# State-space layer with spiking layer on one core: ScalarE's next decay ahead of its weighing of the third tile

## The reference

```python
dA = jnp.exp(dt_t[:, :, None] * A)          # A: one number for each of the 16 states
h = dA * h + dB[:, None, :] * x_t[:, :, None]
y = jnp.einsum('bdn,bn->bd', h, C_t) + Dskip * x_t
```

## Time and profile before

| | |
|---|---|
| median of 3 runs | 5144.43 us |
| the profiled execution | 5153.22 us |
| its span, first to last instruction | 5151.5 us |
| mean granted TensorE clock, share of full | 0.872 |
| VectorE busy | 4268.4 us (83%) |
| GpSimd busy | 4212.7 us (82%) |
| TensorE busy, matmul | 3777.7 us (73%) |
| ScalarE busy | 3045.5 us (59%) |

### The profile page before, as it was taken

How to read it: one execution, slowest core, us unless ns; L and a number is a source line. 1 busy time by engine, 2 the same in 40 slices (tenths; PEclk the granted TensorE clock), 3 DMA queues, 4 the chain that set the end, 5 groups by cost and what they waited for, 6 DMA issues and landing times.

```text
span 5151.5 us, 73020 instructions
## 1 busy us (share of the span) xinstructions
PE 3777.7 (73%) x20244; PEld 2377.5 (46%) x20244; DVE 4268.4 (83%) x3342; ACT 3045.5 (59%) x3906; POOL 4212.7 (82%) x3338
## 2 busy tenths in 40 slices
PE   4677777777777777777777777777777777777765
PEld 1444444444444444444444444444444444444443
DVE  0888888888888888888888888888888888888894
ACT  2566675656656566565665566665666566665552
POOL 1889898878888788887888779888898888888892
PEclk8899888888988889888889888888988898889977
DMA  2212112221222212221222212211221122212210
GB/s 68 77 51 79 57 51 68 69 75 48 63 61 69 67 45 74 59 70 57 62 62 67 60 54 74 63 57 57 74 68 49 57 77 62 60 48 72 63 38 19
DMA packets 189403, 315.20 MB, mean 61 GB/s; under 512 B 51992, under 2 KB 164120, under 8 KB 188960
## 3 DMA queue, kind: packets, MB, share of 16 engines
q1 hardware_dynamic: 188960, 310.06, 20.2%
HBM read 171.87 MB, written 20.05 MB: 37 GB/s over the span
## 4 chain that ended last, share of the span: by engine, by line
PE 24%; issue 22%; DVE 21%; ACT 17%; POOL 11%; SPq 2%; DMA 1%; DVEq 1%; POOLq 0%; ACTq 0%
DVE st L918 15%; PE ht L1038 9%; POOL st L528 8%; ACT decay L674 6%; PE work L1015 4%; PE work L1123 3%; DVE y L901 2%; SPq L402 2%; ACT L660 2%; ACT L815 1%; ACT weighed L685 1%; PE work L1111 1%; PE work L1065 1%; POOL xb L582 1%; PE work L1104 1%
## 5 line engine op out<-in xcount | busy, mean ns | idle before, releaser
L918 DVE TENSOR_TENSOR_SCAN st<-decay,st 128x1536 f32<-128x1536 f32 x768 | 2573.8, 3351 | 328.9 <-ACT decay L674 276.7
L528 POOL TENSOR_TENSOR st<-xc,bbc 128x1536 f32<-128x1536 f32 x768 | 2659.5, 3463 | 75.6 <-DMA bbc<-brow 70.4
L1038 PE MATMUL ht<-ident,st 128*128 128x128 f32 x9216 | 1442.6, 312 | 595.2 <-DVE y L901 581.6
L674 ACT ACTIVATE decay<-dt,neg_a 128x1532 f32<-128x1532 f32 x768 | 1182.3, 1539 | 1063.7 <-DVE st L918 1063.0
L1038 PEld LDWEIGHTS ht<-ident,st 128*128 128x128 f32 x9216 | 1226.1, 162 | 874.8 <-DVE y L901 582.6
L573 POOL TENSOR_TENSOR y<-y,weighed 128x512 f32<-128x512 f32 x768 | 1016.7, 1324 | 474.7 <-ACT weighed L685 468.6
L901 DVE SCALAR_TENSOR_TENSOR y<-ht,ct,y 128x512 f32<-128x512 f32 x1536 | 1067.0, 735 | 42.6 <-PE ht L1038 40.5
L685 ACT ACTIVATE weighed<-ht,ct 128x512 f32<-128x512 f32 x768 | 526.0, 685 | 467.9 <-PE ht L1038 465.8
L1015 PE MATMUL work<-tri,conv_w 96*32 96x384 f32 x4608 | 500.5, 575 | 126.4 <-issue 74.5
L1065 PE MATMUL work<-xn,win 128*128 128x480 f32 x768 | 373.3, 612 | 40.1 <-POOL xn L509 36.4
L1070 PE MATMUL work<-xn,win 128*128 128x384 f32 x768 | 329.8, 581 | 20.3 <-ACT xb L660 19.1
(11 more groups left out here) (91 smaller groups left out, 3543.5 us busy)
## 6 DMA issues: line engine op xcount, KB each, us to landing
bbc<-brow SPq DMA_DIRECT2D x192, 768.0 KB, 4.4
tri<-xhp SPq DMA_DIRECT2D x2304, 50.0 KB, 2.0
xin<-in_x_dram SPq DMA_DIRECT2D x48, 384.0 KB, 3.3
out_dram<-ot SPq DMA_DIRECT2D x48, 384.0 KB, 4.0
brow<-xp SPq DMA_DIRECT2D x48, 24.0 KB, 1.5
win<-in_L_conv_W_in_dram SPq DMA_DIRECT2D x1, 1024.0 KB
wo<-in_L_conv_W_out_dram SPq DMA_DIRECT2D x1, 512.0 KB
w1s<-in_L_conv_W_dram SPq DMA_DIRECT2D x1, 256.0 KB, 3.2
```

The source lines that it names most:

```text
L528: u = g.tensor_tensor(slot, xc[:, kq % 2, :, :], bbc[:, piece_slot(kq, p), n % PIECE, :].unsqueeze(1).to_broadcast([P, DC, T]), ALU.mult)
L674: a.activation(decay[:, :, 1:], dt[:, (k + ahead) % 2, :, 1:], ACT.Exp, scale=neg_a[:, n:n + 1]).then_inc(s_dec, 1)
L918: v.tensor_tensor_scan(state, decay[:, :, :].rearrange("p c t -> p (c t)"), state, 0.0, ALU.mult, ALU.add).then_inc(s_scan, 1)
L1038: last = t.transpose(ht[:, m, c * P:(c + 1) * P], st[:, j, c, m * P:(m + 1) * P], ident[:, :])
```

## The change

In each step ScalarE's call `next_decay(s)` moves from behind the two weighing calls to ahead of them. It stays behind the early evacuations and ahead of the late ones. No instruction is added or removed, and the lists of the other engines are the same.

```diff
                     if s == 12 and PRE2 in do:
                         normalise_input()
+                    next_decay(s)
                     if s >= Y_LAG and main:
                         weigh(s - Y_LAG, 0)
                     if s < Y_LAG and post:
                         weigh(NS - Y_LAG + s, 1)
-                    next_decay(s)
                     for kind, name in late:
                         if kind in do:
                             evacuate(name, kind)
```

## The result

The changed kernel takes 5361.94 us (median of 4 runs, 5352.25 to 5378.45), the kernel before, on the same chips, 5145.53 us. The ratio is 1.042, 95% interval 1.039 to 1.046. The forecast was 5335 us; the change costs 216 us where 190 were expected. Its profiled execution has a span of 5350.5 us.

The account below looks back on a forecast made before the run. VectorE (83% busy) and GpSimd (82%), which every state passes through, were taken to bound the kernel. An estimated 4.0 us for each of 47 block heads, 188 us, on 5153.2 us, less 8.8, gave 5335 us; range 5215 to 5450.

Parts of the forecast that it names:

- The sign and the mechanism: Slower, chance 0.92: the weighing stands behind the decay, delaying GpSimd's sum and the scan input queued behind it.
- The marks that I named: Profile signs: weighing 1.47 us after each decay, fewer decay waits, new waits on GpSimd's lines 528, 535 and its sum.
- well over 1000: GpSimd's wait for ScalarE's weighing was to grow from 468.6 us to more than 1000 us.
- my 3.8: Cost in us of the block worked through: 1.3 + 2.6 + 1.3 - 3.4 + 0.9 + 1.1, with +0.9 for late evacuations.
- the 4.0 us for all blocks: Estimated mean cost per block, between 1.5 and 6.5 us; with 47 block heads, 188 us.
- The loop of 10.60 us for two plain scans: Plain steps: decay, weighing, GpSimd's sum, carry and scan input take 10.60 us per two scans, where it was 9.94.
- The three gaps up to scan 6: Three plain gaps after the block's head, at 10.60 us for two, add 1.3 us.
- The head, 1.3 + 2.6 us: Block start: scan 1 is 1.3 us late behind state 15's sum; scan 3 loses 2.6 more behind the small normalising instructions.
- The stall that gives back 3.4 us: At TensorE's last convolution group, scan 7 is only 1.8 us late instead of 5.2, so 3.4 us come back.
- The tail, 1.1 us: Block end: state 11's sum and scan 14 move by 1.47 us, scan 15 gets part back: +1.1 us.
- The lock: VectorE's line 927 against GpSimd's scan inputs: 51 us back or 66 us cost, left out of the sum.
- the kind case: Rival: all 21 long instructions of line 927 shrink, giving 51 us back, 5282 us; chance 0.15.

Follow-up runs that it names:

- the middle steps: The kernel before, with ScalarE's decay ahead of the weighing in steps 2 to 10 of each block alone; 5126.77 us, ratio 0.9955.

## Why the prediction was right, and where its terms were off

*The sign and the mechanism* were right. The late weighing holds GpSimd's sum, and the next scan input stands behind it. The marks that I named are in the profile: the weighing 1.48 us behind the decay (2682.53 and 2684.01), the statistics that wait for the sum, scans that wait for lines 528 and 535, decay waits down. The same order with only the sum moved is 213 us faster, which shows the mechanism apart from the waits' names. One mark failed in size: GpSimd's wait for the weighing rose to 832.8 us, in 521 places, not "well over 1000". Why it stays below is not shown.

*The number* was helped by luck. In the block of the earlier trace rows the terms are measured at 1.4 + 3.1 + 1.4 - 3.5 + 1.0 + 1.4 = 4.7 us, with some rounding, against my 3.8, and the mean block k = 0 costs 3.6. But the 4.0 us for all blocks were an estimate without a sum behind it, and they hold (4.1) only because lines 873, 881, 884 and 927 give back 12 to 31 us in each of k = 1 to 4 over the eight images. Without that the blocks cost 3.6, 4.2, 6.5, 7.7, 6.6 and 4.7 us, for the stall of blocks k = 0 is missing in k = 2 to 4.

*The loop of 10.60 us for two plain scans* is measured at 5.67 + 4.96 = 10.63 us. I took it for steps of 5.3 us; it shows as a wait in every second step. The three gaps up to scan 6 cost 1.4 us in this block, as forecast (1.3), but over all blocks gaps 3 to 5 together give 15 us back: line 881 returns 22 there, and the stall of blocks k = 5 another 19.

*The head, 1.3 + 2.6 us.* Measured in that block: 8.15 - 6.78 = 1.4 and 12.99 - 9.93 = 3.1 us. The excess in the second is the step from the last small instruction (2695.93 and 0.20 us) to ScalarE's first of the three (2696.60), 0.47 us, for which I had nothing. In the mean of blocks k = 0 the two are 1.2 and 2.7. Over all blocks, gaps 0 and 2 cost 59 + 96 us, and gap 1 gives 15 back. Undone, the head returns 145, and alone it costs 114, so it is half to two thirds of the result.

*The stall that gives back 3.4 us.* In the block of the earlier trace rows the gap of 8.5 us is gone (now 5.0), in the mean of blocks k = 0 gap 6 gives back 2.6 us, and over all blocks 30. But the run with the head in the old order did not bring it back. That it hangs on when the first convolution group starts is therefore not shown, and the middle steps give it back too.

*The tail, 1.1 us,* was too small. Gap 13 costs 74 us, gap 14 gives 12 back and gap 15 costs 7: 69 us, 1.5 us for each block, and the old order in steps 11 to 13 returns 57. In the block of the earlier trace rows it is 2.17 us at gap 13 and 1.4 with the two behind it. I had the sum 1.47 us later; it comes 2.07 later, 8.51 us after scan 12 (2750.18) where it was 6.44. ScalarE's work of step 12 is itself late, behind the weighing of the step before: its line 781 starts 4.88 us after scan 12, where it was 4.27. I also left out the other thing behind the gates, the output projection. The rows of steps 12 and 13:

```profile
2758.69 1.26 POOL L573 TENSOR_TENSOR y<-y,weighed 128x512 f32<-128x512 f32 x1 [1.07 <-ACT weighed L685]
...
2761.68 3.45 PE L1104 MATMUL work<-xb,wo 128*128 128x384 f32 x8
...
2762.22 3.44 POOL L528 TENSOR_TENSOR st<-xc,bbc 128x1536 f32<-128x1536 f32 x1
...
2765.38 0.62 DVE L950 SCALAR_TENSOR_TENSOR img<-work,bo,img 128x384 f32 x1 [2.75 <-PE work L1104]
2765.91 3.35 DVE L918 TENSOR_TENSOR_SCAN st<-decay,st 128x1536 f32<-128x1536 f32 x1
```

Scan 14 starts right behind VectorE's addition to the image, which waited 2.75 us for that projection. But the scan input alone would have let it start at 2762.22 + 3.54 = 2765.76, 0.15 us earlier. So here either would have held the scan, and the projection adds little; VectorE's wait for it over the span rose from 68.2 to 118.7 us.

*The lock,* which I left out of the sum, is the largest term of its own that was missing. Line 927 fell from 135.4 us to 84.1 in the changed kernel, the whole 51 us that I had as the kind case, and line 884 fell from 67.9 to 45.4:

```profile
L927 DVE SCALAR_TENSOR_TENSOR dt<-xb,dt 128x1536 f32<-128x1536 f32 x48 | 84.1, 1751 | 83.6 <-ACT dt L704 83.6
...
L873 DVE SCALAR_TENSOR_TENSOR volt<-ob,volt 128x768 f32<-128x768 f32 x48 | 75.5, 1572 | 5.3
L881 DVE SCALAR_TENSOR_TENSOR ob<-volt,img 128x768 f32<-128x768 f32 x48 | 69.7, 1452 | 0.2
L884 DVE SCALAR_TENSOR_TENSOR volt<-volt 128x768 f32<-128x768 f32 x48 | 45.4, 947 | 0.0
```

The four lines gave 71 us back, and the result still came out 26 us above the forecast's 190. So the waits cost some 290 us, about 100 more than I had (268 by the profiled executions), and the lock hid most of that error: two misses of opposite sign. The Trainium skill (SBUF — State Buffer, "SBUF: two separate sides") says that a VectorE instruction with two SBUF inputs and a GpSimd one that reads SBUF exclude each other. The runs agree: line 927 takes 4.01 us at the mean where GpSimd is let run ahead, 1.75 where it is held.

## What to carry to other kernels

When an instruction moves behind another wait, price what is queued behind its consumer on the consumer's engine, around the whole loop and back; ScalarE was 59% busy and had slack, and the loss arose on GpSimd, which was 82% busy and writes what the scan needs next. Read the shortest and longest of an instruction of fixed size: if they are far apart (1.76 and 4.22 us here), see what the other engines have under way when a long one begins. A change of timing will move such lengths, and holding the other engine back can be worth more than the reordering. Two moves that cancel (the middle steps, at -20 us) need each to be tested with the other's effect taken away.

## What was not expected

Waits on GpSimd in at most three steps of a block, which remove no work, make the kernel before 2.3% faster (5034 us). Moving GpSimd's sum one step later, so that it runs ahead with its scan inputs, makes it 0.9% slower, although the scan then hardly ever waits for GpSimd: the four lines of VectorE grow from 346 to 424 us. An engine that runs ahead is not free where another's instructions stand still for its own.
